# Fused mixture-of-experts and attention kernel: rows of x, a probability turn and the last sum rearranged in the last batch

## The reference

```
xn = layernorm(x)                                     # x: 4 batches x 1024 tokens x 512, f32
s  = softmax_causal(q k^T / sqrt(512)) @ v @ o_proj + xn   # q, k, v from layernorm(xn)*gamma+beta
f  = shared expert(xn) + top-2 of 8 experts(xn)       # gated silu MLPs
g  = silu(f)
out = x + s * g
```

## Time and profile before

| what | us |
|---|---|
| median of 3 runs | 1151.23 (1150.7 to 1157.34) |
| the profiled execution's own time | 1151.93 |
| its span, first to last instruction | 1150.2 |
| PE busy in the span | 1130.9 (98%) |
| DVE busy | 572.2 (50%) |
| ACT busy | 473.4 (41%) |
| POOL busy | 420.7 (37%) |

### The profile page before, as it was taken

One profiled execution on the slowest core, in us unless ns is written; L12 is line 12 of the kernel. 1 busy time (PEld: TensorE's weight loads), 2 busy tenths in 40 slices (PEclk: granted clock), 3 DMA queues, 4 the chain that ended last, 5 costly groups with the idle time before them and its releaser, 6 DMA issues. The chain is left out here.

```text
span 1150.2 us, 21220 instructions
## 1 busy us (share of the span) xinstructions
PE 1130.9 (98%) x6598; PEld 627.0 (55%) x6599; DVE 572.2 (50%) x1236; ACT 473.4 (41%) x859; POOL 420.7 (37%) x656
## 2 busy tenths in 40 slices
PE   8899999999999999999999999999999999999997
PEld 4555555555555555555555555554454454444454
DVE  7876666767469231112211122112477367367467
ACT  5544344444332232223322333224654645555643
POOL 1333233332400222222222222212755754764763
PEclk9999999999999999999999999999999999999999
DMA  9988999989533598988998788875876777766364
GB/s 283 240 208 216 239 242 221 232 203 235 137 76 68 120 197 199 209 201 200 202 202 190 178 175 184 179 170 153 169 181 172 167 160 189 151 160 184 110 155 120
DMA packets 365003, 209.31 MB, mean 182 GB/s; under 512 B 304308, under 2 KB 314816, under 8 KB 364936
## 3 DMA queue, kind: packets, MB, share of 16 engines
q1 hardware_dynamic: 354104, 172.76, 64.1%
q0 software_dynamic: 10800, 35.69, 12.2%
q10 hardware_dynamic: 32, 0.02, 0.0%
HBM read 89.44 MB, written 46.01 MB: 118 GB/s over the span
## 5 line engine op out<-in xcount | busy, mean ns | idle before, releaser
L706 PE MATMUL pair<-arena 128*128 (+2 forms) x3240 | 506.2, 313 | 0.2 <-issue 0.2
L706 PEld LDWEIGHTS pair<-arena 128*128 128x128 f16 x3240 | 316.2, 98 | 182.9 <-issue 1.3
L1638 DVE SCALAR_TENSOR_TENSOR arena<-pair,slot_unit,arena 128x352 f32<-128x352 f32 x71 | 41.5, 584 | 268.9 <-ACT arena L1528 209.5
L713 PE MATMUL bank<-arena 128*128 x639 | 149.3, 379 | 0.0
L1528 ACT ACTIVATE arena<-pair,slot_unit 128x352 f32<-128x352 f32 x71 | 39.4, 555 | 205.5 <-PE pair L706 175.7
L1245 POOL COPY arena<-token_of 128x1 uint32 (+1 forms) x71 | 13.0, 184 | 267.4 <-issue 106.7
L1932 PE MATMUL pair<-arena 128*128 128x512 f16 (+3 forms) x576 | 97.9, 326 | 1.3 <-ACT arena L2000 1.2
L713 PEld LDWEIGHTS bank<-arena 128*128 128x128 f16 x639 | 62.5, 98 | 66.2
L1945 PE MATMUL bank<-arena 128*128 128x512 f16 x411 | 93.5, 379 | 0.0
L1247 POOL DMA_INDIRECT arena<-xn_rows,arena x71 | 70.8, 998 | 55.6 <-POOL arena L1245 54.0
L1912 PE MATMUL bank<-arena 128*128 128x512 f16 x384 | 86.1, 379 | 0.0
(11 more groups left out here) (205 smaller groups left out, 1357.1 us busy)
## 6 DMA issues: line engine op xcount, KB each, us to landing
slot_rows<-arena SPq DMA_DIRECT2D x71, 256.0 KB
arena<-in_L_attn_x_dram SPq DMA_DIRECT2D x64, 256.0 KB, 3.4
xn_rows<-arena SPq DMA_DIRECT2D x32, 260.0 KB, 2.5
shared_rows<-arena SPq DMA_DIRECT2D x32, 256.0 KB
arena<-shared_rows SPq DMA_DIRECT2D x32, 256.0 KB
out_dram<-arena SPq DMA_DIRECT2D x31, 256.0 KB, 2.9
arena<-in_L_ffn_wg_dram SPq DMA_DIRECT2D x32, 176.0 KB, 3.1
arena<-in_L_ffn_wu_dram SPq DMA_DIRECT2D x32, 176.0 KB, 3.3
```

What stands on the lines that cost most here:

```text
L706: last = pe.matmul(bank[:, 0:width], xt[:, a, c, :], weights(c, b, col, width), start=(c == 0 and i == 0), stop=(c == KC - 1 and i == 2))
L713: last = pe.matmul(bank[:, :], ht[:, a, c, :], weights(c, b), start=(start and c == 0 and i == 0), stop=(stop and c == HC - 1 and i == 2))
L1638: v.scalar_tensor_tensor(sbuf[u], u_banks[u][:, 0:H], slot_unit[u][:, 1:2], sbuf[u], ALU.mult, ALU.mult).then_inc(slot_h_ready, 1)
```

## The change

- Buffers `x` and `s` get eight slots instead of four. In the last batch the eight rows of x are loaded and normalised early: `normal(24)` to `normal(27)` in groups 5, 9, 11 and 13, `normal(28)` to `normal(31)` in steps 0 to 3, behind `p_high`. The added bias row (`shift_row`) goes with them: groups 6, 10, 12 and 14, and steps 0 to 3, behind `p_low`. The four loads of x for tiles 28 to 31 go into SP's queue in the early part of the batch, with a wait for `normal` of the tile four earlier.
- In SP's queue the store of tile 27 moves from before `turn_probs(31)` to behind it.
- The tanh of the last tile moves from step 7 to step 6 of ACT, and its g (`end(31)` on DVE) to before `combine(29)`.
- The last tile's product and sum are regrouped: `base_last` makes s*g/(2 S_Q) + x ahead, and each half of `combine_last` then has two operations (PSUM * inv * g, and times 0.5/S_Q plus base) instead of three.

```diff
-            X_AHEAD = 4
-            S_AHEAD = 4
+            X_SLOTS, X_SEMS = 8, 4
+            LAST = (B - 1) * QT
+            NORMAL_GROUP, NORMAL_STEP = {5: 0, 9: 1, 11: 2, 13: 3}, {0: 4, 1: 5, 2: 6, 3: 7}
+            SHIFT_GROUP = {6: 0, 10: 1, 12: 2, 14: 3}
...
                 def load_x(t):
-                    wait(sp, res_ready, t - X_AHEAD + 1)
+                    wait(sp, res_ready, t - X_SLOTS + 1)
+                    wait(sp, xn_made, t - X_SEMS + 1)
...
                 def pass_on(t):
                     store_tile(t)
-                    if t + X_AHEAD < NT:
-                        load_x(t + X_AHEAD)
+                    if t + X_SEMS < NT - X_SEMS:
+                        load_x(t + X_SEMS)
...
                             load_shared(b * QT + {3: 2, 4: 3, 6: 4}[j])
+                        if b == B - 1 and j in (3, 4, 6, 7):
+                            load_x(NT - 4 + {3: 0, 4: 1, 6: 2, 7: 3}[j])
...
-                        if n > 2:
+                        if t == NT - 1:
+                            pass_on(t - 4)
+                        if n > 2 and t != NT - 2:
                             pass_on(t - 3)
...
                 def normal(t):
-                    wait(act, res_ready, t - S_AHEAD + 1)
+                    wait(act, res_ready, t - X_SLOTS + 1)
...
-                        if g_ in (0, 2, 5, 9):
-                            t = b * QT + {0: -2, 2: -1, 5: 0, 9: 1}[g_]
-                            if t >= 0:
-                                normal(t)
+                        if g_ in (0, 2) and b > 0:
+                            normal(b * QT + {0: -2, 2: -1}[g_])
+                        if g_ in NORMAL_GROUP and (g_ < 10 or b == B - 1):
+                            normal(b * QT + NORMAL_GROUP[g_])
...
                             p_high(t)
-                        if n > 3:
+                        if b == B - 1 and n in NORMAL_STEP:
+                            normal(b * QT + NORMAL_STEP[n])
+                        if n > 3 and b < B - 1:
                             normal(t - 2)
                         if n in BEGIN_STEP:
                             begin(b * QT + BEGIN_STEP[n])
-                        if n in END_STEP:
+                        if t == NT - 2:
+                            end(NT - 1)
+                        if n in END_STEP and t != NT - 1:
                             end(b * QT + END_STEP[n])
-                normal(NT - 2)
-                normal(NT - 1)
...
+                def shift_row(t):
+                    row = c["s", t % X_SLOTS]
                     dve.wait_ge(xn_made, t + 1)
                     v.tensor_tensor(row, row, bias_rows, ALU.add).then_inc(s_shifted, 1)
...
+                def combine_first(t):
+                    dve.wait_ge(exp_done, t + 1)
+                    v.reciprocal(c["inv", t % 2], sums[:, t % 4:t % 4 + 1]).then_inc(inv_ready, 1)
+                    if t < LAST:
+                        shift_row(t)
...
+                def base_last(t):
+                    row, x_row = c["s", t % X_SLOTS], c["x", t % X_SLOTS]
+                    dve.wait_ge(s_shifted, t + 1)
+                    dve.wait_ge(g_made, t + 1)
+                    v.scalar_tensor_tensor(row, row, 0.5 / S_Q, g[:, t % QT, :], ALU.mult, ALU.mult).then_inc(base_made, 1)
+                    dve.wait_ge(x_loaded[t % X_SEMS], (t // X_SEMS + 1) * 16)
+                    dve.wait_ge(base_made, 1)
+                    v.tensor_tensor(x_row, row, x_row, ALU.add).then_inc(base_made, 1)
...
                     for n, cols in enumerate(halves):
                         dve.wait_ge(pv_done, t + n + 1)
-                        v.scalar_tensor_tensor(row[:, cols], last_banks[n][:, cols], c["inv", u][:, 0:1], row[:, cols],
-                                               ALU.mult, ALU.add).then_inc(s_made, 1)
+                        v.scalar_tensor_tensor(row[:, cols], last_banks[n][:, cols], c["inv", u][:, 0:1], g[:, t % QT, cols],
+                                               ALU.mult, ALU.mult).then_inc(s_made, 1)
                         dve.wait_ge(s_made, t + n + 1)
-                        v.scalar_tensor_tensor(row[:, cols], row[:, cols], 0.5 / S_Q, g[:, t % QT, cols], ALU.mult, ALU.mult
-                                               ).then_inc(o_made, 1)
-                        dve.wait_ge(o_made, t + n + 1)
-                        v.tensor_tensor(res[:, cols], row[:, cols], x_row[:, cols], ALU.add).then_inc(last_added, 1)
+                        v.scalar_tensor_tensor(res[:, cols], row[:, cols], 0.5 / S_Q, base[:, cols], ALU.mult, ALU.add
+                                               ).then_inc(last_added, 1)
...
                             combine(b * QT + WEIGH_GROUP[g_])
+                        if b == B - 1 and g_ in SHIFT_GROUP:
+                            shift_row(LAST + SHIFT_GROUP[g_])
                         if g_ in G_GROUP:
                             end(b * QT + G_GROUP[g_])
...
                             p_low(t)
+                        if b == B - 1 and n in NORMAL_STEP:
+                            shift_row(LAST + NORMAL_STEP[n])
                         if n > 2 and t != NT - 2:
                             combine(t - 3)
...
+                end(NT - 1)
                 combine_first(NT - 3)
                 combine(NT - 3)
-                end(NT - 1)
+                base_last(NT - 1)
                 combine_first(NT - 2)
                 combine(NT - 2)
                 combine_first(NT - 1)
```

More of the change, by code:

```diff
@@ L1682, in stage4 @@
                     c[name, u], at = carve(at, shape, dt)
-            for u in range(X_AHEAD):
+            for u in range(X_SLOTS):
                 c["x", u], at = carve(at, [D], F32)
-            for u in range(S_AHEAD):
+            for u in range(X_SLOTS):
                 c["s", u], at = carve(at, [D], F32)
@@ L1711, in stage4 @@
             pv_done = sem("pv_done")
-            x_loaded = [sem(f"res_x_loaded{u}") for u in range(X_AHEAD)]
+            x_loaded = [sem(f"res_x_loaded{u}") for u in range(X_SEMS)]
             f_loaded = [sem("shared_loaded0"), sem("shared_loaded1")]
@@ L1727, in stage4 @@
             last_added = sem("last_added")
+            base_made = sem("base_made")
             halves = [slice(n * D // 2, (n + 1) * D // 2) for n in range(2)]
@@ L1767, in load_x @@
                 def load_x(t):
-                    wait(sp, res_ready, t - X_AHEAD + 1)
-                    r, u = place(t) * P, t % X_AHEAD
-                    sp.dma_start(c["x", u], X_FLAT[r:r + P, :]).then_inc(x_loaded[u], 16)
+                    wait(sp, res_ready, t - X_SLOTS + 1)
+                    wait(sp, xn_made, t - X_SEMS + 1)
+                    r = place(t) * P
+                    sp.dma_start(c["x", t % X_SLOTS], X_FLAT[r:r + P, :]).then_inc(x_loaded[t % X_SEMS], 16)
                 def store_tile(t):
@@ L1862, in finish @@
                     wait(pool, res_stored[u], t // 2 * 16)
-                    pool.tensor_tensor(c["res", u], c["s", t % S_AHEAD], c["x", t % X_AHEAD], ALU.add).then_inc(res_ready, 1)
+                    pool.tensor_tensor(c["res", u], c["s", t % X_SLOTS], c["x", t % X_SLOTS], ALU.add).then_inc(res_ready, 1)
                 gather(0)
@@ L2026, in normal @@
                     p = place(t)
-                    act.wait_ge(x_loaded[t % X_AHEAD], (t // X_AHEAD + 1) * 16)
-                    wait(act, res_ready, t - S_AHEAD + 1)
-                    nc.scalar.activation(c["s", t % S_AHEAD], c["x", t % X_AHEAD], ACT.Identity, scale=rstd[:, p:p + 1],
+                    act.wait_ge(x_loaded[t % X_SEMS], (t // X_SEMS + 1) * 16)
+                    wait(act, res_ready, t - X_SLOTS + 1)
+                    nc.scalar.activation(c["s", t % X_SLOTS], c["x", t % X_SLOTS], ACT.Identity, scale=rstd[:, p:p + 1],
                                          bias=shift[:, p:p + 1]).then_inc(xn_made, 1)
@@ L2096, in end @@
                                            ).then_inc(g_made, 1)
[L2098 to L2102, removed]
+                def shift_row(t):
+                    row = c["s", t % X_SLOTS]
                     dve.wait_ge(xn_made, t + 1)
                     v.tensor_tensor(row, row, bias_rows, ALU.add).then_inc(s_shifted, 1)
+                def combine_first(t):
[3 more added lines that the diff above has]
+                        shift_row(t)
                 def combine(t):
-                    u, row = t % 2, c["s", t % S_AHEAD]
+                    u, row = t % 2, c["s", t % X_SLOTS]
                     dve.wait_ge(inv_ready, t + 1)
@@ L2117, in combine, with combine_last @@
                                            ).then_inc(o_made, 1)
-                def combine_last(t):
-                    u, row, res, x_row = t % 2, c["s", t % S_AHEAD], c["res", t % 2], c["x", t % X_AHEAD]
-                    dve.wait_ge(inv_ready, t + 1)
+                def base_last(t):
+                    row, x_row = c["s", t % X_SLOTS], c["x", t % X_SLOTS]
```

(9 more changed lines are left out.)

## The result

The changed kernel took 1156.13 us (median of 20 runs, 1153.23 to 1160.47), the kernel before 1153.01 (20 runs, 1149.95 to 1157.85). The ratio is 1.0031, 95% interval 1.0019 to 1.0042: slower by 3.6 us, between 2.2 and 4.8. The forecast was a sum of +2.65 us, called "no change"; the measurement tells it from no change.

What follows compares the result with a forecast made beforehand. PE was taken as the bound, with a soften-exponential-high-low chain through DVE beside it in the last batch. Terms 4.3 + 0 - 1.65 gave +2.65 us on 1151.93, 1154.6; less 0.7 for the median, 1153.9, range 1148.4 to 1156.4.

Steps and rivals of the forecast that it cites:

- Groups 5 to 14: Rows normalised and shifted early in the last batch: soften(25) 0.85 us late, between 0.1 and 1.4.
- Steps 1 and 2: shift_row(29) before soften(26) and shift_row(30) before soften(27) on DVE: +0.7 and +0.6 us.
- Step 3: shift_row(31) pushes combine(24) behind POOL's sum; soften(28) +2.15 us, or +0.5 if not caught. N: start of normal(31).
- Steps 4 to 7: Removed rows give the chain nothing; begin(31) 0.72 us earlier may make soften(30) 0.85 later or earlier; taken as 0.
- The turn: turn_probs(31) ahead of tile 27's store: low part's turn 1.25 us sooner, PE freed, end brought nothing by itself.
- The tail: DVE from p_low(31) on, with shifts gone and the last sum regrouped: -1.65 us, between -2.3 and -0.95.
- The close: From DVE's last operation to the end of the span; the prediction added nothing for it.
- "Hidden": Rival: moved rows fit DVE's and ACT's idle time, only the tail shortens, by 2.3 us to 1148.9; chance 0.28.
- "Stores": Rival: late landing stores hold up combine_last at the end, 0.7 us of the tail's gain goes, 1154.6; chance 0.09.
- "Clock": Rival: more PE idle time drops its clock from 2.4 to 1.2 GHz, 1163 to 1190 us; chance 0.02.

Runs made afterwards that it cites:

- the cut sums: Changed kernel with POOL's two expert-row sums for the last two tiles cut to one column of 512; ratio 1.0007 to the kernel before.
- The kernel with the early begin: Kernel with all rows in gaps, but normal(31) behind begin in step 5, so begin(31) starts earlier; 60.50 us from group 12 to DVE's last operation, no ratio.
- the end alone: Kernel before with eight slots, turn first, early tanh and g, two-operation last sum, rows of x normalised and shifted where they were; ratio 1.0025.
- The kernel with all rows in gaps: Changed kernel with rows 26 to 31 normalised in steps 0 to 5, shifted in steps 1 to 6 between soften and p_low; ratio 0.9987, again 0.9984.

## Why the prediction was right and where it failed

*What bounds.* Right: the chain of soften, exponential, high and low part runs beside PE, and DVE work inserted behind `p_low` lengthens it. Placing four rows on the other side of `p_low` shows it (2.91 us).

*Groups 5 to 14*: +0.85 predicted at `soften(25)`, 0.58 measured; PE idle 0.30, not 0.4 to 0.9. By themselves they are worth 0.47.

*Steps 1 and 2*: +0.7 and +0.6 predicted; 0.71 and 0.60 measured (1.29 - 0.58, 1.89 - 1.29).

*Step 3*: +2.15 predicted, 2.05 measured (3.94 - 1.89). L2131 started at N + 2.30 (N is 1115.85), 0.19 behind POOL's sum, and ended at N + 3.93; N + 2.47 and N + 3.94 were worked out. That POOL's sums make these two operations long is shown by the cut sums: both fall to 0.69. The split was less good. I put 0.5 on the insertion and the rest on the collision; the rows give 1.12 and 0.93.

*Steps 4 to 7*: I took 0, the middle of two ends. Measured +0.82 at `soften(30)`, of which `p_low(30)` gave 0.40 back: +0.42. The worked-out order of starts (POOL at 1122.95, L2116 at 1123.28) had already told which end it was; the same reading that I trusted in step 3 I did not trust here. The kernel with the early begin shows it by itself: +0.83 and +0.44.

*The turn*: right, it frees PE and brings the end nothing (L equal to 0.01 us).

*The tail*, up to DVE's last operation: -1.65 predicted (its items as listed add to -1.68), -2.21 measured, just inside the range given. From `soften(31)` to the end of `p_low(31)` it gained 0.80 (6.22 to 5.42), where I had 0.4: `p_low` took 1.68 and not 2.17, and DVE reached it sooner. The rest, 1.41 (11.56 to 10.15), was worked out as 1.25. The attribution to single operations was less sound: the end alone, with the rows left where they were, costs 1.76 us. The gain comes with the three shifts that left the end; the regrouped sum alone has none.

*The close*: the working ends with DVE's last operation and puts what follows at nothing, without a reason. Measured +0.88. The end of the span kept its distance from POOL's `finish(30)`, not from DVE, so 0.88 of the tail's 2.21 us never reached it.

*The sum*: +2.65 predicted; +2.15 measured to DVE's last operation and +3.03 to the end of the span. The terms missed by -0.27, +0.01, 0, -0.10, +0.42, -0.56 and +0.88, which is +0.38. That the sum came so near is in part luck: steps 4 to 7 and the close, both put at nothing, were set off by the groups and the tail.

*The step that failed* is the last, "this is 'no change'": I put the bound at 1%, and twenty runs of each gave an interval of 0.12% to either side, which excludes both 1 and a difference under 2.2 us. My own sum had the sign and the size: the mechanism was right, and the step from it to a verdict was wrong. The terms under it that were mis-sized are the close (0 for 0.88), the tail (-1.65 for -2.21) and steps 4 to 7 (0 for 0.42). The chances should have followed the sum and its worked-out ends, mostly above zero.

*The signs.* Of what was to show the prediction right, `soften(28)` came 3.94 us late (some 4), the last low turn went out 0.03 us after `p_low(31)` (within 0.1) and DVE ended 10.15 us after it (some 10). L2131 took 1.63 where about 1.3 was said, and PE idled 1.46 before `scores(28)` where about 2 was said.

*The rivals.* "Hidden" fell: the changed kernel does not hide the rows. The idea was sound and its placement not. The kernel with all rows in gaps has its 2.3 us nearly in L (2.21), but 1.32 to the end of the span. "Stores" did not occur; no wait of DVE for a store is among the waits of the changed kernel. "Clock": the granted clock was 1.00 in every stretch of the last batch to 1152 us, when PE's last matmul had ended, so not this either.

*What stays open.* The ratio says 3.6 us (2.2 to 4.8), and 3.1 when it was measured again; the last batch to the end of the span says 3.03 and 3.10. The 0.5 us left of the first lie well inside its interval, and the slots cost nothing (their kernel measured 0.9987). Open is what holds the end of the span 5.6 us behind `finish(30)`: no run moved `finish(30)` by itself.

## What to carry to other kernels

When work is moved off a tail, look at each engine's idle time by its place in the order: the gap between `soften` and `p_low` took a 0.68 us row free in every step, the place right behind `p_low` cost it in full and more. If DVE and POOL both work from SBUF, list the starts of both: an operation that leads POOL by 0.2 us may lose 0.9 when it is pushed behind, and so may one whose rival starts earlier. And a wait on the busiest engine is worth its length only if the engine behind it would have been ready: here 1.23 us of PE were worth 0. When a part is judged by its own length, let that length run to the end of the span, or check that the rest stays the same: here a shorter DVE tail of 2.21 us was worth 1.32.

## What the runs showed of the hardware

DVE and POOL took turns where both had operations queued that read two SBUF buffers. In step 3 of the changed kernel POOL's sums ended at 1119.23 and 1120.90, and DVE's L2131 and L2105 each ended 0.55 us behind one of them (1119.78 and 1121.45); their 1.63 and 1.75 us are mostly waiting. The Trainium skill (SBUF — State Buffer, "Who interferes with whom") states the exclusive lock; the cut sums agree with it (0.69 us as soon as POOL's sum is small). It also says that a DVE operation with at most one SBUF input, outside the two-port modes, does not contend with GpSimd. The trace agrees: L2152, which reads PSUM and one SBUF buffer, took 0.48 us beside `finish(30)` (POOL from 1151.80 to 1153.06) and 0.47 without it, and L2155 behind it, with both inputs in SBUF, took 0.99 instead of 0.42 and ended 0.28 after POOL.

Not expected: how exactly the last batch repeats. L is 62.26 to 62.28 in four profiles with DVE's old end and 64.42 in two of the changed kernel, while the start of group 12 lies anywhere from 1084.2 to 1090.9 us over the fourteen profiles. A difference of 0.05 us in the last batch can be read from one profile, where 20 runs of each kernel give the total to 1.3 us to either side.
